# A two-layer graph network on one core: the ELU's arithmetic and the skip's relu from VectorE and ScalarE to GpSimd, and new step lists on all engines

## The reference

```python
h = maximum(layernorm(x), 0)
q, k, v = heads(h @ Wq + bq), heads(h @ Wk + bk), heads(h @ Wv + bv)      # 6 heads of 64
probs = softmax(q @ k.T / 8 + where(adj, 0, -9e15))
x = x + (probs @ v) @ Wf + bf

h = maximum(layernorm(x), 0)
hh = einsum('bnd,ade->bane', h, W)                                        # 12 heads of 32
attn = tanh(hh) @ w_src + (tanh(hh) @ w_dst).T
attn = softmax(where(adj, leaky_relu(attn, 0.2), -999))
out = elu(concat_heads(attn @ hh + b))
gate = sigmoid(h @ H_w.T + H_b)
x = x + gate * out + (1 - gate) * h
```

## Time and profile before

| | us |
|---|---|
| median of 3 runs | 1313.34 |
| lowest and highest run | 1312.08, 1313.35 |
| span of the profiled execution, first to last instruction | 1309.3 |
| PE busy in that span | 1265.7 |
| ACT busy | 1251.5 |
| DVE busy | 1209.1 |
| POOL busy | 913.2 |

### The profile page before, as it was taken

The page is one execution under the profiler, slowest core; times in us unless marked ns, Lnnn a source line. Parts: engine busy times, 40 slices in busy tenths (PEclk is TensorE's granted clock), DMA queues, the critical chain, the costliest instruction groups (busy, mean ns, idle before and its releaser), DMA issues.

```text
span 1309.3 us, 33375 instructions
## 1 busy us (share of the span) xinstructions
PE 1265.7 (97%) x10511; PEld 918.9 (70%) x10511; DVE 1209.1 (92%) x4401; ACT 1251.5 (96%) x3701; POOL 913.2 (70%) x1106
## 2 busy tenths in 40 slices
...
DMA packets 29854, 33.74 MB, mean 26 GB/s; under 512 B 10481, under 2 KB 29681, under 8 KB 29681
## 3 DMA queue, kind: packets, MB, share of 16 engines
...
## 4 chain that ended last, share of the span: by engine, by line
PE 88%; ACT 3%; DVE 3%; POOL 2%; DMA 1%; issue 1%; SPq 1%; POOLq 0%; DVEq 0%; ACTq 0%
PE job L623 27%; PE pt L696 18%; PE job L635 14%; PE unit L670 7%; PE job L718 7%; PE job L764 6%; PE job L611 4%; PE unit L687 3%; PE job L773 2%; ACT p L874 1%; DMA xb<-in_x_dram 1%; PE job L619 1%; POOL prod L1282 1%; ACT pT L884 1%; DVE y L1051 1%
## 5 line engine op out<-in xcount | busy, mean ns | idle before, releaser
L874 ACT ACTIVATE p<-y,min 128x256 f32<-128x256 f32 x768 | 394.1, 539 | 0.9 <-DVE min L1125 0.8
L1119 DVE SCALAR_TENSOR_TENSOR unit<-unit,s,dst 128x256 f32<-128x256 f32 x768 | 335.8, 482 | 14.0 <-issue 1.7
L696 PE MATMUL pt<-ident,p 128*128 128x128 f32 x2304 | 331.5, 275 | 12.3 <-ACT p L874 7.1
L623 PE MATMUL job<-w,h 128*128 128x384 f16 x1728 | 311.1, 326 | 1.8 <-DVE h L1024 1.7
L696 PEld LDWEIGHTS pt<-ident,p 128*128 128x128 f32 x2304 | 268.3, 142 | 42.9 <-ACT p L874 14.0
L1125 DVE CUSTOM_DVE_ANT_0 y<-unit,mask 128x256 f32<-128x256 f32 x768 | 290.5, 414 | 0.0
L1260 POOL TENSOR_SCALAR p<-p,rec 128x256 f32<-128x256 f32 x384 | 178.7, 481 | 123.3 <-DVE rec L1058 122.9
L623 PEld LDWEIGHTS job<-w,h 128*128 128x128 f16 x1728 | 168.6, 98 | 97.3 <-DVE h L1024 2.5
L884 ACT ACTIVATE pT<-pt 128x512 f32<-128x512 f32 x384 | 232.3, 624 | 1.6 <-PE pt L696 1.6
L635 PE MATMUL job<-h,w 128*128 128x256 f16 x1728 | 216.4, 274 | 2.3 <-DVE h L1024 2.1
L830 ACT ACTIVATE p<-y,min 128x256 f32<-128x256 f32 x384 | 191.0, 503 | 13.8 <-PE pt L696 7.9
...
## 6 DMA issues: line engine op xcount, KB each, us to landing
...
```

What stands on the lines that cost most here:

```text
L623: last = mm(bank[:, 0:H], rows[:, i, c, t * P:(t + 1) * P], w16[:, w, j, c, :], start=n == 0, stop=(c, i, j) == (NC - 1, *TERMS[-1]))
L696: last = nc.tensor.transpose(pt_ps[u % 2][:, (2 * hh + kt) * P:(2 * hh + kt + 1) * P], probs[:, u % 3, hh, kt * P:(kt + 1) * P], ident[:])
L874: last = op(p1[:, u % 3, hh, :], y1[:, u % YB, hh, :], ACT.Exp, bias=min1[:, u, hh:hh + 1], scale=-1.0, accum_out=sum1[:, t, h:h + 1])
L1119: V.scalar_tensor_tensor(leaky[:, hh * T:(hh + 1) * T], bank[:, hh * T:(hh + 1) * T], s8[par][:, t, h:h + 1], dst5[:, c % 2, hh, :], ALU.a ...
```

## The change

It does five things.

1. The ELU. `ELU_RELU` is gone from ACT. 1 is subtracted from the bias row in advance, so that o is one less than before; `ELU_BIAS` on POOL, after adding the bias, also writes min(o, -1) and max(o, -1), each a tensor_scalar with two constants; ACT takes exp(min + 1); `FINISH`, now on POOL, is their sum and then its product with the gate.
2. The skip's relu `SKIP_H` is on POOL, as min with 3e38 and max with 0. The scale 1/XS is folded into `ungate`.
3. In `SCORE_SUM`, the two casts to bf16 on DVE become additions of a tile of zeros.
4. The last batch's halves are finished on DVE by a step `LAST_ROWS` of three instructions for each half.
5. All step lists are new. The waits that they need change with them: the two PSUM banks of the transposes alternate over both layers and each has a semaphore of its own, `EXP0` and `EXP1` wait only for the transposes that read their own buffer, `wait_taken` takes the latest use of each bank, and some waits on read buffers are added (`STATS0`, `AGGREGATE1`, `RSTD0/1`, `OUT_T`, `SKIP`, `ELU_BIAS`, `LOAD_ADJ`).

```diff
 ORDERS = {
     "PE": steps("""
-        B PV1 0, P QK 0, L LN_T0 0, B PT1 9, B PT1 10, P QK 1, A GATE 1, B PT1 11, P QK 2, L LN_T0 1, P PT0 0,
+        L LN_T0 0, P QK 0, B PV1 0, P QK 1, B PT1 9, L LN_T0 1, B PT1 10, A GATE 1, B PT1 11, P PT0 0, P QK
...
     "SP": steps("""
-        L LOAD_X 0, C STORE 0, L LOAD_ADJ 0
+        L LOAD_X 0, P LOAD_ADJ 0, C STORE 0
     """),
...
+        def prob_bank(b, step, u):
+
+            n = n_t.before(b, step, u)
+            return pt_ps[n % 2], s_pT[n % 2], n // 2
...
             def transpose_probs(b, step, u, probs):
-                if n_t.some_before(b, step, u, 1):
-                    pe.wait_ge(s_pT, n_t.before(b, step, u, 1))
+                bank, evacuated, used = prob_bank(b, step, u)
+                if used:
+                    pe.wait_ge(evacuated, used)
...
             def exp0(b, par, u):
                 act.wait_ge(s_y0, n_y0.after(b, "SCORES0", u))
-                if n_t.some_before(b, "PT0", u, 2):
-                    act.wait_ge(s_t, n_t.before(b, "PT0", u, 2))
+                if u >= 3:
+                    act.wait_ge(s_t, n_t.after(b, "PT0", u - 3))
+                elif b.ref >= 1:
+                    act.wait_ge(s_t, n_t.after(b.back(1), "PT0", u + 3))
...
+            def elu_exp(b, par, _):
                 if b.ref == NB - 1:
-                    act.wait_ge(s_half["bias"], 1)
-                    op(o1m[:, 0, :], o1[:, 0, :], ACT.Relu, scale=-1.0).then_inc(s_half["exp"], 1)
-                    act.wait_ge(s_half["exp"], 1)
-                    op(o1m[:, 0, :], o1m[:, 0, :], ACT.Exp, scale=-1.0).then_inc(s_half["exp"], 1)
-                    act.wait_ge(s_ob, n_ob.after(b, "ELU_BIAS"))
-                    op(o1m[:, 1, :], o1[:, 1, :], ACT.Relu, scale=-1.0).then_inc(s_om, 1)
-                else:
-                    act.wait_ge(s_ob, n_ob.after(b, "ELU_BIAS"))
-                    op(o1m[:], o1[:], ACT.Relu, scale=-1.0).then_inc(s_om, 1)
-
-            def elu_exp(b, par, _):
-                act.wait_ge(s_om, n_om.after(b, "ELU_RELU"))
+                    act.wait_ge(s_half["negative"], 1)
+                    op(o1m[:, 0, :], o1m[:, 0, :], ACT.Exp, bias=one[:]).then_inc(s_half["exp"], 1)
+                act.wait_ge(s_om, n_om.after(b, "ELU_BIAS"))
                 rows = slice(1, NT) if b.ref == NB - 1 else slice(0, NT)
-                op(o1m[:, rows, :], o1m[:, rows, :], ACT.Exp, scale=-1.0).then_inc(s_oe, 1)
+                op(o1m[:, rows, :], o1m[:, rows, :], ACT.Exp, bias=one[:]).then_inc(s_oe, 1)
...
-                V.tensor_copy(nd_parts[:, :, 0, :], nd[:]).then_inc(s_sd, 1)
+                V.tensor_tensor(nd_parts[:, :, 0, :], nd[:], zero[:], ALU.add).then_inc(s_sd, 1)
...
-                V.tensor_copy(nd_parts[:, :, 1, :], nd_r[:]).then_inc(s_nd, 1)
+                V.tensor_tensor(nd_parts[:, :, 1, :], nd_r[:], zero[:], ALU.add).then_inc(s_nd, 1)
...
-                    V.scalar_tensor_tensor(o1m[:], o1[:], 0.0, o1m[:], ALU.max, ALU.add).then_inc(s_fin, 1)
...
-                    V.scalar_tensor_tensor(y[:], o1m[:], -1.0, gate[par][:], ALU.add, ALU.mult).then_inc(s_fin, 1)
+                V.scalar_tensor_tensor(o1m[:, t, :], o1[:, t, :], -1.0, o1m[:, t, :],
+                                       ALU.max, ALU.add).then_inc(s_half["elu"], 1)
+                dve.wait_ge(s_half["elu"], t + 1)
+                V.tensor_tensor(y[:, t, :], o1m[:, t, :], gate[par][:, t, :], ALU.mult).then_inc(s_half["gated"], 1)
+                dve.wait_ge(s_half["gated"], t + 1)
+                V.tensor_tensor(y[:, t, :], y[:, t, :], xskip[par][:, t, :], ALU.add).then_inc(s_half["rows"], 1)
...
-                G.tensor_scalar(ungate[:], gtanh[:], -0.5, 0.5, ALU.mult, ALU.add).then_inc(s_gate, 1)
+                G.tensor_scalar(ungate[:], gtanh[:], -0.5 / XS, 0.5 / XS, ALU.mult, ALU.add).then_inc(s_gate, 1)
+
+            def skip_h(b, par, _):
+                pool.wait_ge(s_norm1, n_norm1.after(b, "NORM1"))
+                if b.ref >= 1:
+                    pool.wait_ge(s_ungate, n_ungate.after(b.back(1), "SKIP"))
+                G.tensor_scalar(hskip[:], xn[1][:], 3.0e38, 0.0, ALU.min, ALU.max).then_inc(s_hskip, 1)
...
+                    pool.wait_ge(s_ob, n_ob.after(b, "ELU_BIAS"))
+                    G.tensor_scalar(o1m[:], o1[:], -1.0, -3.0e38, ALU.min, ALU.max).then_inc(s_om, 1)
+                    pool.wait_ge(s_om, n_om.after(b, "ELU_BIAS"))
+                    G.tensor_scalar(o1[:], o1[:], 3.0e38, -1.0, ALU.min, ALU.max).then_inc(s_op, 1)
+
+            def finish(b, par, _):
+                pool.wait_ge(s_op, n_op.after(b, "ELU_BIAS"))
+                pool.wait_ge(s_oe, n_oe.after(b, "ELU_EXP"))
+                G.tensor_tensor(o1m[:], o1[:], o1m[:], ALU.add).then_inc(s_fin, 1)
+                pool.wait_ge(s_fin, n_fin.after(b, "FINISH", k=1))
+                pool.wait_ge(s_gate, n_gate.after(b, "GATES"))
+                if b.ref >= 1:
+                    pool.wait_ge(s_out, n_out.after(b.back(1), "STORE"))
+                G.tensor_tensor(y[:], o1m[:], gate[par][:], ALU.mult).then_inc(s_fin, 1)
```

381 lines of the change are left out of this document (196 added, 185 removed).

## The result

| | before | changed | span of the profiled execution |
|---|---|---|---|
| median of 7 runs each, one chip | 1312.98 us | 1316.50 us | 1309.3, then 1314.9 |

The changed kernel takes 1.0036 of the time of the kernel before (95% interval 1.0027 to 1.0045): **slower by 0.36%**, 3.5 us against the median and outside the bound of 0.2%. Run again beside other kernels on another chip, the ratio was 1.0050 (1.0035 to 1.0064). The forecast was 3.5 us faster. In these runs the time is 1.8 to 2.1 us over the span of the same execution (1303.27 us for a span of 1301.2, for instance), so the profiled execution before was probably one of the shorter ones, at about 1311.2; that would be why the spans are 5.6 apart and the medians 3.5. What follows is counted in spans, from one trace of each kernel.

The account below looks back on a forecast made before the run. PE's own work was taken to bound the steady-state loop. Loop +3.5, start -4.3 and end -2.7 sum to -3.5 us, giving 1309.8 us from a median of 1313.34, with a range from 1300 to 1321.

Parts of the forecast that it names:

- What bounds the kernel: Steady state: PE's own work sets the time, busy 1040.00 of 1040.00 us; others matter only through PE's waits or step order.
- ACT and DVE, taken at nothing: Loop: ACT loses 0.86 us a batch and DVE 2.3, worth nothing because PE's unbroken work covers it.
- PE's order: Loop: one array shape change fewer, 0.06 us, and some 0.2 of small waits gone; turn 38.95 to 38.68.
- POOL's load: Loop: five new instructions, 6.1 us a batch, bring POOL from 28.3 to 34.4 us a turn; it fits.
- The new wait of DVE on POOL: Loop: `OUT_SUM` holds `SCORE_SUM`'s first addition about 1.1 us, delaying PE 0.40 at `PT0 1`; turn 39.08, +3.5 us over 27 turns.
- Casts: `SCORE_SUM`: additions in place of casts are held alike by POOL, so worth nothing.
- Start: Before the loop: earlier first product and earlier loads of x save 4.3 us, bounds 0 and -7.6.
- End: Past 1220 us: `ELU_RELU` savings 1.5, earlier exponential 0.4, `SCORE_SUM` no longer held 0.8; -2.7 us, bounds 0 and -5.
- The last rows: Very end: POOL's bias and min replace ACT's relu, DVE takes two halves; taken at 0, from -0.3 to +0.3.
- The rivals: Three alternatives: slack holds, 1301 us, chance 0.27; POOL late, 1320, 0.23; start and end gain nothing, about 1314, 0.10.
- the slack: Loop rival: 0.65 us of slack keeps PE unheld at `PT0 1`, turn 38.68 to 38.75, total 1301 us; chance 0.27.
- The late GpSimd: Loop rival: POOL's new work ahead of `SCORE_PROD` delays PE, at 0.4 us a turn +10.8 on the forecast, 1320; chance 0.23.

Follow-up runs that it names:

- experiment one: Changed kernel with `OUT_SUM` moved in POOL's loop list from behind `NORMP0 0` to directly behind `SCORE_PROD`: 0.9964 of the kernel before, turn 38.74 us.
- experiment eight: On top of experiment one, `FINISH` put on VectorE instead of GpSimd, at two places: 1.0170 and 1.0254 of the kernel before, turns 39.80 and 40.01 us.
- experiment nine: Against experiment one, PE's loop order: `PV1 0` ahead of both `QK` and `LN_T0 0`, 1.1645; `QK 0` ahead of `LN_T0 0`, 1.0081 of the kernel before.
- second trace: The changed kernel run again unaltered, beside other kernels on one chip: 1.0050 of the kernel before, turn 39.08 us.
- experiment five: Changed kernel with the third-last batch's `FINISH` on GpSimd also waiting for the last batch's `SCORE_SUM`: 1.0015 of the kernel before.
- k1: The kernel of experiment one: changed kernel with `OUT_SUM` directly behind `SCORE_PROD` in the loop, 0.9964 of the kernel before.
- k16: Changed kernel with only the two GpSimd edits of experiment one and experiment five together: 0.9941 of the kernel before, 1302.99 us against 1310.84.
- k9: The kernel of experiment five with the ending lists of PE, ScalarE and VectorE taken from the kernel before: 1.0076 of the kernel before.
- k10: k9 with `ELU_EXP` of the third-last batch back at its later place, joined with experiment one: 0.9944 of the kernel before.

## Why the prediction was wrong, point by point

- **What bounds the kernel**: right. In the loop only what PE does or waits for counted; experiment one changes no engine's work and gives 9.4 us.
- **ACT and DVE, taken at nothing**: wrong in its reason. in the new lists PE's unbroken work does not cover 1.9 us more of VectorE in one piece: with `FINISH` there, PE waits 0.7 us a turn at one place and 1.2 at the other (experiment eight). The 52 us of free time in the stretch say nothing of a piece put in at one point.
- **PE's order**: the sum was nearly right, 38.68 forecast and 38.74 measured without the hold, but its parts were not, and that the total came out is luck. The one change of shape is worth 0.15 (experiment nine), not 0.06, which leaves 0.06 of the 0.21 for the small waits in place of 0.2.
- **POOL's load**: right. The new instructions took 0.83 and 1.82; POOL was busy for 33.6 us a turn (893.56 in 1040), where 34.4 was worked out. It was late by 0.2 ahead of `SCORE_PROD`, worth 0.12 a turn, which my count from the end of `HEADS` left out.
- **The new wait of DVE on POOL**: right in mechanism, place and about in size. Hold 1.0 us (forecast 1.1), cost 0.34 a turn (0.40 taken, 0.3 to 0.6), turn 39.08 (39.08), the loop +3.1 in 23 turns, +3.5 in 27 (+3.5). The exact match of the turn is two errors of 0.06 that cancel, this one and the one of PE's order. It came out ahead of `PV1 1`, which the prediction named second.
- **Casts**: right, nothing.
- **Start**: -2.4 up to batch 6 with three turns of +0.13 in it, so about -2.8 where -4.3 was taken (-1.9 by the second trace); inside its bounds.
- **End**: this step failed. I had -2.7, with bounds 0 and -5, and it is +4.9 from the tanh at 1188. I used the rows at 1235, where `OUT_SUM` had held `SCORE_SUM`, and took 0.8 as the gain. That hold did go (0.18 us each at 1235.67), and the stretch up to the last tanh is 0.8 us shorter. But I didn't lay the two lists side by side once more for the last batch, where POOL's list has `MASK1 0 0, FINISH 0 2` just as VectorE comes to `SCORE_SUM 0 0`. The same count as in the loop would have given it: the mask ends at 1269.7, VectorE's reductions at 1269.9. Of the 5.8 us lost behind the last tanh, this hold is 3.7 by the spans of experiment five, and about 3 by the ratios (0.21% there, 0.23% between k1 and k16). For the remaining 2 to 3 us two things are seen. The last product at half the clock is on the chain of the changed kernel, at 3.42 us for 1.93; in the runs where it was fast again (k9, k10) the whole order of the ending was the old one, and nothing was gained. The late `FINISH` of the second-last batch costs 1.3 us, but only in the kernels with the old order. How much each takes in the changed kernel stays open.
- **The last rows**, taken at nothing: right. From the end of the last product to the last instruction it is 9.3 us in both.
- **The rivals**: the slack didn't hold. The late GpSimd was there, but it cost 0.12 us a turn and not the 0.4 that this rival needed. None of the rivals was the case that came, a second hold in the ending; the range had no term for an end that loses. With -2.8 + 3.5 + 4.9 for -4.3 + 3.5 - 2.7 the sum by its own steps is +5.6, which is what the spans show; the three terms are read from the same two traces, so this only says that none is left out.

The Trainium skill (GPSIMD Engine Reference, section Engine selection) had the sign by its rule. Experiments one and eight show that the rule isn't the reason: with `OUT_SUM` out of the way, twice the time per instruction was paid in free time in the loop, and having `FINISH` on GpSimd is worth 1.06 us a turn in these lists (38.74 against 39.80). The other rule (SBUF — State Buffer, section Who interferes with whom) is the one that decided: its exclusive lock is in the loop at 1.17 us and in the ending at 1.75 and 1.67. The advice of the same page (section Summary: rules for kernel authors), to schedule whichever is off the critical path, is what experiments one and five do.
